# A normalised cross-attention block with paired scores and GpSimd sums, and matmuls issued into known waits of TensorE

## The reference

```python
def _qk_norm(a):
    var = jnp.mean(jnp.square(a), axis=-1, keepdims=True)
    return a * jax.lax.rsqrt(var + EPS)

def _attn(xq, xkv, wq, wk, wv, wo, rep):
    q, k, v = ...
    q, k = _qk_norm(q), _qk_norm(k)
    k, v = jnp.repeat(k, rep, axis=2), jnp.repeat(v, rep, axis=2)
    attn = softmax(einsum('bqhd,bkhd->bhqk', q, k) / sqrt(64))
    return einsum('bhqk,bkhd->bqhd', attn, v).reshape(...) @ wo
```

## Time and profile before

| | us |
|---|---|
| median of 3 runs (2018.36 to 2020.66) | 2020.42 |
| the profiled execution's own time | 2019.28 |
| its span, first to last instruction | 2017.4 |
| PE busy in the span | 1763.7 (87%) |
| DVE busy | 1333.8 (66%) |
| ACT busy | 866.4 (43%) |
| POOL busy | 629.4 (31%) |

### The profile page before, as it was taken

The page is one execution under the profiler, slowest core; times in us unless marked ns, Lnnn a source line. Parts: engine busy times, 40 slices in busy tenths (PEclk is TensorE's granted clock), DMA queues, the critical chain, the costliest instruction groups (busy, mean ns, idle before and its releaser), DMA issues.

```text
span 2017.4 us, 34290 instructions
## 1 busy us (share of the span) xinstructions
PE 1763.7 (87%) x10630; PEld 1229.5 (61%) x10630; DVE 1333.8 (66%) x3366; ACT 866.4 (43%) x2513; POOL 629.4 (31%) x732
## 2 busy tenths in 40 slices
PE   5979998899988878888879999887888979998988
PEld 4746665689966665555755555573445845555567
DVE  5866777311148868888566767795778966566665
ACT  3745554333345624564334444343333444444421
POOL 2325555310032345676300000130001344454443
PEclk9989999799998988998889999897998989999989
DMA  4100000579841001101100020101001000000200
GB/s 170 37 24 17 11 4 16 179 285 327 318 163 43 0 1 40 39 30 58 68 16 16 8 70 0 52 1 63 0 0 69 6 1 19 16 11 12 74 1 19
DMA packets 37011, 115.16 MB, mean 57 GB/s; under 512 B 3344, under 2 KB 23728, under 8 KB 29728
## 3 DMA queue, kind: packets, MB, share of 16 engines
q1 hardware_dynamic: 34352, 107.33, 15.2%
q0 software_dynamic: 2544, 6.43, 1.0%
HBM read 99.34 MB, written 14.40 MB: 56 GB/s over the span
## 4 chain that ended last, share of the span: by engine, by line
PE 45%; issue 18%; DVE 16%; POOL 13%; ACT 5%; DMA 2%; POOLq 0%; DVEq 0%; SPq 0%; ACTq 0%
POOL arena L2047 10%; PE ps L1017 7%; PE ps L1057 4%; PE ps L830 4%; PE ps L1162 4%; PE ps L882 3%; PE ps L1174 3%; PE ps L936 3%; PE ps L825 3%; PE ps L956 2%; ACT arena L1290 1%; PE ps L900 1%; PE ps L810 1%; DVE arena L1727 1%; DVE negmax L1690 1%
## 5 line engine op out<-in xcount | busy, mean ns | idle before, releaser
L2047 POOL TENSOR_TENSOR arena<-arena,rinv 112x375 f32<-112x375 f32 (+1 forms) x448 | 371.2, 830 | 474.1 <-DVE rinv L1695 463.4
L900 PEld LDWEIGHTS ps<-cst,arena 112*125 112x125 f32 (+1 forms) x1408 | 186.5, 182 | 175.9 <-issue 86.6
L900 PE MATMUL ps<-cst,arena 112*125 112x112 f32 (+1 forms) x1408 | 246.0, 292 | 45.0 <-POOL arena L2047 39.6
L1290 ACT ACTIVATE arena<-ps,negmax 112x375 f32<-112x375 f32 (+1 forms) x384 | 190.6, 502 | 159.3 <-DVE negmax L1690 159.0
L1704 DVE COPY arena<-ps 125x336 f32<-125x336 f32 x384 | 190.4, 496 | 45.2 <-PE ps L900 44.0
L2100 POOL TENSOR_TENSOR w_split_sb<-wml,w_split_sb 128x512 fp32r<-128x512 f32 (+1 forms) x40 | 46.1, 1152 | 526.9 <-ACT w_split_sb L1356 525.1
L1690 DVE TENSOR_REDUCE negmax<-ps 112x1 f32<-112x375 f32 (+1 forms) x288 | 158.1, 549 | 66.3 <-PE ps L872 59.2
L1017 PE MATMUL ps<-h_split_sb,w_split_sb 128*128 128x448 f32 x768 | 180.1, 384 | 17.0 <-DVE h_split_sb L1570 6.2
L1290 ACT ACTIVATE arena<-arena,negmax 112x112 f32<-112x112 f32 (+1 forms) x256 | 125.4, 491 | 142.7 <-DVE negmax L1679 94.0
L1017 PEld LDWEIGHTS ps<-h_split_sb,w_split_sb 128*128 128x128 f32 x768 | 150.9, 198 | 34.9 <-DVE h_split_sb L1570 12.9
L825 PE MATMUL ps<-wat,arena 128*125 128x256 f32 (+1 forms) x608 | 151.5, 387 | 8.8 <-ACT arena L1234 7.3
(11 more groups left out here) (221 smaller groups left out, 3172.5 us busy)
## 6 DMA issues: line engine op xcount, KB each, us to landing
wml<-in_wm_L_moe SPq DMA_DIRECT2D x21, 1028.0 KB, 7.2
wml<-in_wm_L_moe SPq DMA_DIRECT2D x21, 1024.0 KB, 7.9
craw<-in_ctx SPq DMA_DIRECT2D x32, 375.0 KB
wml<-in_wm_L_m SPq DMA_DIRECT2D x3, 3072.0 KB, 14.0
wat<-in_wa_L_ca SPq DMA_DIRECT2D x2, 2560.0 KB, 9.4
wml<-in_wm_L_m SPq DMA_DIRECT2D x2, 2048.0 KB, 9.9
keys_hbm<-arena SPq DMA_DIRECT2D x8, 375.0 KB
arena<-keys_hbm SPq DMA_DIRECT2D x8, 375.0 KB
```

Source lines behind the costliest of these rows:

```text
L900: last = nc.tensor.transpose(ps[0:blk.kp, T_BANK + s % blk.t_banks, o:o + S], buf[:, i * blk.nk + q * blk.kp:i * blk.nk + (q + 1) * blk.kp ...
L1290: last = go(probs[0:S, s % blk.nprobs, i * nk:(i + 1) * nk], src[:, i * nk:(i + 1) * nk], ACT.Exp, scale=-1.0 if blk.mask == "input" else ...
L2047: pool.tensor_tensor(p3, p3, r3, ALU.mult).then_inc(scaled, 1)
```

## The change

It has three parts. First, L2_ca joins `PAIRS`: it scores two units at a time. Second, `add_chunks` moves from VectorE to GpSimd, with a wait on `av_done` added before it writes `psums`, and `weigh` waits for the exponentials before its matmuls with the values and for the sums only before the matmuls with ones. Third, `keep_busy` issues fp32 matmuls of the 128x128 identity with itself into a PSUM bank that nobody reads then; the table `WARM` says where and how many, 214 in all.

```diff
+WARM = {
+    "L1_sa": dict(tail={1: 7}, tokens=5),
+    "L1_m1": dict(second=8, out=12),
+    "L1_ca": dict(scores=14, tail={3: 9}),
+    "L1_m2": dict(first=6, second=8, out=12),
+    "L2_ca": dict(QT0=20, tail={1: 22}),
+    "L2_m1": dict(second=9, out=12),
+    "L2_sa": dict(QT0=24, tail={0: 10}),
+    "L2_m2": dict(second=9, out=12),
+    "L3_ca": dict(tail={3: 6}),
+    "L3_m": dict(second=9),
+}
-PAIRS = ("L0_ca", "L1_ca", "L3_ca",)
+PAIRS = ("L0_ca", "L1_ca", "L2_ca", "L3_ca")
...
+            def keep_busy(bank, times):
+                for _ in range(times):
+                    nc.tensor.matmul(ps[:, bank, 0:P], ident, ident, start=True, stop=True)
...
                         if i == 0:
+                            if isinstance(m, int) and m == 0 and "QT0" in warm:
+                                pe.wait_ge(out_done, st["out"])
+                                keep_busy(O_BANK, warm["QT0"])
                             pe.wait_ge(qk_ready, count(st["qk"], 1, m, 1))
...
-                    elif blk.kc > 1:
-                        pe.wait_ge(summed, count(0, 4, b, g + 1))
                     else:
-                        pe.wait_ge(exped, count(st["unit"], units, b, g + 1))
+                        pe.wait_ge(exped, count(st["unit"], units, b, (g + 1) * gu))
...
                     if blk.keys_first:
+                        if blk.kc > 1:
+                            pe.wait_ge(summed, count(0, 4, b, g + 1))
                         for z in range(2):
...
+                if "scores" in warm:
+                    keep_busy(O_BANK, warm["scores"])
                 def body(b):
                     for s in steps(b, blk, blk.out_step + 1):
+                        if b == B and s in warm.get("tail", {}):
+                            keep_busy(spare, warm["tail"][s])
...
                             pe.wait_ge(exped, START[n + 1]["unit"])
+                            keep_busy(spare, warm.get("tokens", 0))
                             for b2_ in range(SOON):
                                 turn_tokens(n + 1, b2_)
...
+                keep_busy(5, warm.get("first", 0))
                 for t in range(2 * FC + 2):
                     if t == 2:
                         for b2_ in range(SOON, B // 2):
                             turn_tokens(n, b2_)
+                        keep_busy(5, warm.get("second", 0))
...
                     bank = out_banks(n)[b]
+                    if b == 6:
+                        keep_busy(5, warm.get("out", 0))
...
-                def add_chunks(b, s):
...
-                        elif at and blk.kc > 1:
-                            add_chunks(*at)
...
+                def add_chunks(b, s):
+                    g, q = group_of(blk, s)
+                    if q == 0:
+                        return
+                    pool.wait_ge(exped, count(st["unit"], units, b, s + 1))
+                    new = pT[0:kp, g, q].rearrange("p h s -> p (h s)")
+                    if q == 1:
+                        wait(pool, av_done, count(st["group"], 2, b, g // 2 - 1))
+                        pool.tensor_tensor(psums[0:kp, g], pT[0:kp, g, 0].rearrange("p h s -> p (h s)"), new, ALU.add)\
+                            .then_inc(part_summed, 1)
+                    else:
+                        pool.wait_ge(part_summed, count(0, 4, b, g + 1))
+                        pool.tensor_tensor(psums[0:kp, g], psums[0:kp, g], new, ALU.add).then_inc(summed, 1)
```

More of the change, by code:

```diff
@@ L772, in _ @@
         def _(pe):
+            def keep_busy(bank, times):
+                for _ in range(times):
+                    nc.tensor.matmul(ps[:, bank, 0:P], ident, ident, start=True, stop=True)
             def attention(n):
                 blk, st = BLOCKS[n], START[n]
+                warm = WARM.get(blk.name, {})
+                spare = 7 if blk.out_bank != 7 else blk.w_banks[1]
                 np_, units, gu, lag = len(blk.pieces), blk.units, blk.gu, blk.lag
@@ L2011, in attention @@
                 blk, st = BLOCKS[n], START[n]
-                units, nk = blk.units, blk.nk
+                units, nk, kp = blk.units, blk.nk, blk.kp
                 q3 = qt[0:S].rearrange("p (h d) -> p h d", d=64)
@@ L2058, in body, with body_of_sums @@
                         scale(b, s)
+                def add_chunks(b, s):
[11 more added lines that the diff above has]
+                        pool.tensor_tensor(psums[0:kp, g], psums[0:kp, g], new, ALU.add).then_inc(summed, 1)
+                def body_of_sums(b):
+                    for s in steps(b, blk, 1):
+                        at = lagged(b, s, 1, units)
+                        if at:
+                            add_chunks(*at)
                 if not blk.keys_first:
                     batches(pool, body)
+                elif blk.kc > 1:
+                    batches(pool, body_of_sums)
             def mixture(n):
```

## The result

The changed kernel takes 1981.34 us (median of 4 runs, 1977.45 to 1986.23) against 2020.45: a ratio of 0.9819, 95% interval 0.9802 to 0.9837. Forecast were 1984, between 1966 and 2004, and faster. The profiled execution took 1980.68 us with a span of 1978.9. Here are its lines that answer to those of before.

The account below looks back on a forecast made before the run. TensorE bounds L2_ca's steady batches; at block seams it runs at half clock after waits. Terms -10 - 4.5 - 7.5 - 6 - 8.5 + 0.8 - 1 = -36.7 took 2019.28 to 1982.6, plus 1.1: 1984, range 1966 to 2004.

Parts of the forecast that it names:

- L2_ca's loop: Seven steady batches of L2_ca: paired scores gain 1.4 us each, net of waits, together -10.
- Step (b): L2_ca, QT0's weight loads: VectorE's normalisation shrinks from 8.1 to 7.5 to 7.9; the wait grows about 0.6, to 1.0.
- cost 0: L2_ca's sums on GpSimd: adds of 1.0 cost nothing while 2.3 us of value matmuls cover them.
- 1.2 that is there already: Steady L2_ca batch: of 2.9 us of predicted waits, about 1.2 exists before the change.
- Contention: L2_ca's loop: GpSimd's adds taken to cost VectorE 0, bound 1.0 a batch; rival of contention or waits: 1996, chance 0.12.
- L2_ca's end: Last batch of L2_ca: 1.3 from an earlier start, 1.7 from clock after 22 fillers, 1.5 from pairs: -4.5.
- Ends of MLPs: Four MLP ends: 12 fillers take 2.9 us, fit a wait of 3.31 and keep full clock: -7.5 in all.
- the term of 2.5: Start of L3_ca: eight QP instructions at full clock after 12 fillers at L2_m2's end: -2.5.
- QT0 in L2_sa: Start of L2_sa: -3.5 from 24 fillers before QT0; with -2.5 from L2_m1's end, -6.0 for the stretch.
- Overrun: Rival: fillers begin at low clock, take 0.48 each and outlast their waits: 2056 us, chance 0.07.
- the term of +0.8: Before L1_ca's scores: 14 fillers last 3.3 us against a wait of 2.76, partly over: +0.8.
- Second units: 8 or 9 fillers at MLPs' second units: L3_m -2.9, the other four -1.4 each (half): -8.5.

Follow-up runs that it names:

- the bare kernel: The changed kernel with an empty table of fillers; paired scores and GpSimd sums stay: 1996.52 us, ratio 0.9884.

## Why the prediction was right, and which of its steps weren't

**L2_ca's loop: right in size, wrong in what makes it.** The forecast put the whole -10 on the pairs and 0 on the sums. Pairs alone give 0.18 a batch, sums alone cost 0.26, both together give 1.29. The failed step is where the sums' worth was booked. Step (b) counted the add that leaves VectorE's chain, 0.6 of it, as a part of the pairs, and "cost 0" for the sums asked only whether they come late; so in the forecast the pairs pay by themselves. The length of the chain was right: from VectorE's first operation to QT0 it is 8.1 with the adds and 7.4 without (1105.73 to 1113.15); the forecast had 7.5 to 7.9. But QT0's wait of 1.0 started from 0.58, which is idle time of the weight loads; PE itself didn't wait there in the kernel before:
```profile
1153.63 0.60 PE L837 MATMUL ps<-cst,arena 112*128 112x112 f32 x4
```
With VectorE's adds pairs make the wait 0.97, without them 0.25. That the 1.4 a batch came out near 1.29 is partly luck. The pairs took 2.57 off PE's work and not 3.1, the waits are 1.62 and not 2.9, and of the "1.2 that is there already" the window showed 0.29: three errors of 0.5 to 1.3 that nearly cancel.

**Contention: right for the loop.** The forecast said that unit 5's add meets VectorE in its 1.23 us operation and costs it nothing. DVE and POOL in the steady batch of the changed kernel:
```profile
1105.73 1.23 DVE L1657 TENSOR_TENSOR arena<-arena 112x1024 f32<-112x1024 f32 x1 [2.34 <-ACT arena L1289]
...
1106.29 1.66 POOL L2088 TENSOR_TENSOR arena<-arena 125x448 f32<-125x448 f32 x1 [1.27 <-ACT arena L1313]
...
1116.73 1.15 DVE L1555 TENSOR_SCALAR xn<-X,rstd 112x256 f32 x1
```
The add waits (1.66; others take 1.13), VectorE doesn't; the other victim, `xn` with 1.15 instead of 0.35, isn't waited for. GpSimd's adds are longer than the 1.0 of the forecast, 1.15 and 1.27 in the mean:
```profile
L2088 POOL TENSOR_TENSOR arena<-arena 125x448 f32<-125x448 f32 x32 | 40.3, 1271 | 50.6 <-ACT arena L1313 50.6
L2084 POOL TENSOR_TENSOR arena<-arena 125x448 f32<-125x448 f32 x32 | 36.6, 1145 | 125.6 <-ACT arena L1313 124.3
```
So the rule that the forecast weighed (the Trainium skill, GPSIMD Engine Reference, section 1) agrees with the trace as a mechanism; whether it costs anything is a matter of the order of the work: +0.26 a batch in one kernel, while in this one four more adds a batch cost 0.03.

**L2_ca's end: right in size (-4.0 for -4.5), wrong in cause.** I gave the 22 fillers 3 of it. Kernels without them take 23.2 as well. What the short ends have in common is the late wait of `weigh`: the nine kernels with it take 23.1 to 23.7, also the one with VectorE's sums; the four with the early wait take 25.6 to 29.0, also the one with GpSimd's sums and all fillers, 26.7. There `weigh` still waits for the sums; in the bare kernel the last `weigh` waits 2.18, for `divide`, where it waited 6.53 for the sums. The first line is GpSimd's sums with the early wait, the second the bare kernel:
```profile
1252.95 4.11 PE L957 MATMUL ps<-arena,vz 125*64 125x448 f32 x12 [2.17 <-POOL arena L2088]
...
1266.08 4.17 PE L944 MATMUL ps<-arena,vz 125*64 125x448 f32 x12 [2.18 <-DVE arena L1735]
```
With the early wait and VectorE's sums the fillers did shorten this end, from 27.2 to 25.6; the two don't add. In the changed kernel they even hold `weigh`:
```profile
1252.83 5.18 PE L788 MATMUL ps<-cst 128*128 128x128 f32 x44
...
1257.93 2.48 PE L955 MATMUL ps<-arena,vz 125*64 125x448 f32 x12
...
1262.85 2.94 DVE L1744 RECIPROCAL arena<-ps 128x448 f32<-128x448 f32 x1
```
`weigh` starts straight behind them and is done with its sums at 1261.1, but `divide` starts only at 1262.85, when VectorE is done normalising tokens. So their overrun costs nothing and their clock gives nothing there. L2_m1 behind it took 0.8 more in the run without the 22, but 0.2 more in the one that also left out L2_m1's 9, so a gain there isn't shown either.

**Ends of MLPs: they fit, and the clock follows.** The fillers take 0.24 each, the wait behind them is 0.62, and L2_ca's start gave -7.5 and -6.0 for -6.4:
```profile
1011.51 2.84 PE L788 MATMUL ps<-cst 128*128 128x128 f32 x24
...
1015.20 0.43 PE L1115 MATMUL ps<-cst,arena 128*112 128x128 f32 x2 [0.62 <-DVE X L1903]
```
For L3_ca's start the term of 2.5 was mis-sized: measured -6.7 and -4.1. QP, KT and the first scores before, then the same with the values' projection V ahead of KT in the first profile of the changed kernel, then KT and the first scores in its second:
```profile
1620.92 6.18 PE L830 MATMUL ps<-wat,arena 128*112 128x512 f32 x8 [1.24 <-DVE X L1888]
...
1637.83 0.84 PE L844 MATMUL ps<-cst,arena 125*128 125x125 f32 x6 [2.15 <-DVE arena L1663]
1639.49 1.51 PE L877 MATMUL ps<-arena 64*112 64x375 f32 x4 [0.83 <-ACT arena L1272]
```
```profile
1597.37 3.69 PE L849 MATMUL ps<-wat,arena 128*112 128x512 f32 x8 [1.43 <-DVE X L1903]
...
1603.57 7.17 PE L844 MATMUL ps<-wat,arena 128*125 128x256 f32 x24 [0.90 <-ACT arena L1266]
...
1612.24 0.83 PE L866 MATMUL ps<-cst,arena 125*128 125x125 f32 x6 [0.42 <-DVE arena L1695]
1613.89 0.89 PE L899 MATMUL ps<-arena 64*112 64x375 f32 x4 [0.82 <-ACT arena L1304]
```
```profile
1612.17 0.83 PE L866 MATMUL ps<-cst,arena 125*128 125x125 f32 x6 [1.61 <-DVE arena L1695]
1613.83 1.31 PE L899 MATMUL ps<-arena 64*112 64x375 f32 x4 [0.82 <-ACT arena L1304]
```
QP's 2.5 are there in both. Behind it the two executions part. In the first the clock fell earlier: V took 7.17, where it takes 5.52 before and in the second profile, the wait before KT shrank to 0.42, and the first scores ran at full clock. In the second the wait was 1.61 and the clock fell there as before. The nine profiles with these 12 fillers took 69.0 to 73.3 in this stretch, the four without 74.5 to 76.0. I had priced one stretch at half clock, not how the later falls shift with it.

**QT0 in L2_sa: the step that failed most, -0.8 and -1.6 for -6.** The 2.5 at QP are there (3.66 for 6.15). The 24 fillers also ran at full clock, but ended 1.37 before QT0, and two more waits follow:
```profile
1345.83 5.52 PE L788 MATMUL ps<-cst 128*128 128x128 f32 x48
1352.73 0.99 PE L859 MATMUL ps<-cst,arena 112*128 112x112 f32 x8 [1.37 <-DVE arena L1677]
...
1354.63 0.42 PE L866 MATMUL ps<-cst,arena 112*128 112x112 f32 x1 [0.82 <-issue]
1356.03 1.81 PE L904 MATMUL ps<-arena 128*112 128x448 f32 x2 [0.98 <-ACT arena L1304]
...
1359.05 6.51 PE L849 MATMUL ps<-wat,arena 128*112 128x512 f32 x8 [0.84 <-ACT arena L1260]
```
The clock falls at 1354.6, with the first of these two waits, and the second QP pays what the first gained. With 30 fillers and 4 more, the same piece takes 3.66. But five other kernels that kept the 24 took 57.6 to 58.3 for this stretch, -3.3 to -4.0; so how much of the 2.8 is the placing stays open, and the step was too large by 2 to 5.

**Overrun: the rival happened in small.** In L1_ca and L1_m2 the fillers stand behind the wait, and begin when the clock is about to fall or has fallen:
```profile
778.16 4.79 PE L788 MATMUL ps<-cst 128*128 128x128 f32 x28 [2.55 <-DVE X L1903]
...
968.00 0.60 PE L1030 MATMUL ps<-cst,arena 112*128 112x112 f32 x4 [2.84 <-DVE arena L1556]
968.45 3.28 PE L788 MATMUL ps<-cst 128*128 128x128 f32 x16
```
The 14 take 4.79 instead of 3.3, the 8 take 3.28 instead of 1.9, and the 9 at L1_ca's end 3.31 instead of 2.1: 0.34 to 0.41 each in the mean, on the way to the rival's 0.48, in three places of nineteen. Against the kernel before, the term of +0.8 became +2.2 and +3.6. But the other kernels without fillers took 39.8 to 42.6 for this stretch, and the three that kept the 12 at L1_m1's end but not the 14 (one has 10 ahead of the wait) took 38.5, 38.5 and 39.9; so a cost of the 14 is likely, and its size is open.

**Second units.** L3_m -2.8 (second profile -2.1) for -2.9, L1_m1 -1.4 for -1.4; but -0.6, -0.5 and -0.3 in the other three, with up to 0.8 between kernels that have no filler there. Against the bare kernel L3_m gained 1.5 and 0.7, and L1_m1 2.8. That "half" was too much where the clock before was low for a short part only fits this, but no run separates it.

**What the change doesn't touch.** A steady batch of L3_ca takes 36.9 to 37.0, or 38.2 to 41.3 when a stretch at half clock lies in it, and L2_sa's 19.5, or 21.1 to 22.6. The profile of before had more of these, which gave some 7 of the 38.5 between the spans. The four kernels with sums on VectorE all had 225.5 to 226.0 in L3_ca's seven adds, the nine others 220.2 to 223.4. L3_ca uses none of the moved code. Why this is so wasn't tried and is open, and with it some 5 us of the gain.

## What to carry to other kernels

In these runs fillers worked best where they were issued while the clock was still up and reached to the end of the wait: put them ahead of the wait that lets the clock fall, count the short waits behind it too, and leave them out where another engine sets the end. Late ones aren't always lost: with the 9 at L1_ca's end, slow as they were, its last batch took 26.7 and 27.3, without them 28.7. Where TensorE gets faster in a tight loop, look for the engine that it will wait for next and unload that one in the same change; alone either step can be worth nothing or less. A wait placed as late as the data allows can matter more than which engine does the work: at L2_ca's end it was worth some 3.5 us with GpSimd's sums, the choice of engine under the late wait some 0.5. A total that comes out right says little about its terms: compare stretch by stretch, with more than one execution, and see first how far the stretches of unchanged kernels differ.

## What the runs showed of the hardware that was not expected

VectorE was held for the whole of a GpSimd add that had begun just before: 1.17 us instead of 0.19 for a step of 28 columns beside an add of 1.13, and 1.15 instead of 0.35 for `xn`. The other way round the add was held, 1.66 for 1.13. I had expected operations that slow each other down, not an order in which the first one wins. The Trainium skill (SBUF — State Buffer, Who interferes with whom) calls the port pair that the two engines share an exclusive lock and says of VectorE's two-port modes that whoever issues first gets the pair for the whole instruction, while the other is fully blocked. The trace agrees with such an order in both directions; in which mode these VectorE steps ran no row shows.

One program's stretches at 1.2 GHz aren't the same in each execution: TensorE was busy for 111.0 us at that level in the first profile of the changed kernel and for 118.3 in the second, and the starts of blocks moved by up to 2.6 us. That is why a few filler edits of 1 to 3 us can't be told apart by totals alone.
